# Query columns fetched from device memory in place of a TensorE transpose and a ScalarE copy, in a graph attention kernel

## The chip, the core and the metric

The kernel runs on one core of a Trainium2 chip. The core has five engines that run side by side, each in the order of its own program: TensorE (PE; its weight loads are listed as PEld), VectorE (DVE), ScalarE (ACT), GpSimd (POOL) and SyncE (SP), which here issues all but two of the transfers. They meet through semaphores. The metric is the device time of one execution in microseconds; before the change the median of three runs is 1442.3 us (1441.92 to 1442.65).

## The reference

Two layers over 128 graphs of 128 nodes with 256 features:

```python
h = relu(layernorm(x));  x = x + (adj @ (h @ W0) + b0)
h = relu(layernorm(x))
proj = (h @ fc_w + fc_b) split into 8 heads of 256
q = proj @ q_w + q_b;    k = proj @ k_w + k_b          # one number per node and head
masked = leaky_relu(q + k.T + (1 - adj) * -1e9, 0.01)
out = softmax(masked) @ proj                            # per head
x = x + sigmoid(concat(out) @ fp_w + fp_b + h)
```

All of it is in 32-bit floats. The attention logit of nodes n and m in a head is the sum of a query that depends on n and a key that depends on m.

## The kernel before

The 128 graphs are taken as 64 pairs (J = 2 graphs each). Weights are folded before the loop: `fc_w` and `fp_w` become one matrix `m` per head, so that a pair needs only projections into `gbank` (`project`) and an attention-weighted sum into `ybank` (`attend`). Most products are made of three matmuls on a high and a low part of each operand (helper `split`, L350). For each pair the engines do this:

- TensorE makes a block of 16 key and 16 query rows per pair, and the low part of each, in `kq` (`queries_keys`, L431). ScalarE copies the low part out (`kq_rows`, L1206), VectorE adds high, low and bias into `kq_sb` (`keys_queries`, L784). In `kq_sb` graph j has 8 key rows and 8 query rows from row 32 j on, 128 nodes wide.
- Keys are needed as rows on every partition: SP writes `kq_sb` to device memory (`keys_out`, L248) and reads the key rows back, repeated over all 128 partitions (`keys_in`, L260, 1 MB). GpSimd adds them to the mask (`mask_keys`, L1556).
- Queries are needed as columns, one number per partition and head: TensorE transposes `kq_sb` (`turn_queries`, L437), and ScalarE copies 16 of its columns into `qs` (`queries`, L1213). VectorE adds them to the masked keys and takes the minimum (`mask_min`, L810).
- Then come the slope and the negated exponent (`leaky` L817, `exp` L1226), the reciprocal of the sum (`inverse` L822), `normalise` on GpSimd (L1563), the transpose of the attention weights on TensorE (`transpose_p`, L454), their high and low parts (L1233, L800) and `attend`. `project` is followed by its own high and low parts (`g_high` L1219, `g_low` L793), which free its bank for a later `project`.

The work of neighbouring pairs is interleaved. Its order on every engine is written out by hand: a start (`begin`), a loop body with three pairs a turn (`step` for pair i), and an end (`finish`). In the loop body SP issues `load(i)`, `keys_in(i - 4)`, `store(i - 6)` and `keys_out(i - 3)`. `load` waits until GpSimd has used up the buffer (L1546, L1548). Pair i + 1 gets its key and query rows while pair i is projected, and uses them one body later. Buffers for rows, keys and queries exist three times (U = 3), and key rows go through the three tensors `key_rows0` to `key_rows2`.

Of the kernel before, what the change touches and what calls it, by code (L numbers as in the profile page):

```python
# [10 lines left out]
P = 128  # L11
D = 256
DT = D // P
H = 8
J = 2
# [12 lines left out]
U = 3  # L28
# [12 lines left out]
def gnn_pair(nc, graph, identity, head_mask, row_coef, w0, bias0, fc_wT, fc_b, qk_w, q_b, k_b, fp_w, fp_b, out):  # L41
# [9 lines left out]
    with ExitStack() as ctx:  # L51
# [87 lines left out]
        kq, kqT = bank1[0:2 * HALF, 0:J * P], bank1[:, J * P:J * P + P]  # L139
# [6 lines left out]
        s_loaded, s_stored, s_rows, s_keys = sem("s_loaded"), sem("s_stored"), sem("s_rows"), sem("s_keys")  # L146
        g_ones, g_none, g_qk = sem("g_ones"), sem("g_none"), sem("g_qk")
# [10 lines left out]
        pe_kq, a_kq, v_kq, pe_kqT, a_qs = [sem(n) for n in ("pe_kq", "a_kq", "v_kq", "pe_kqT", "a_qs")]  # L158
# [42 lines left out]
        def _(sp):  # L201
# [42 lines left out]
            def keys_out(p, q):  # L244
                sp.wait_ge(v_kq, p + 1)
                if has(p - 1):
                    sp.wait_ge(s_rows, 16 * p)
                sp.dma_start(key_rows[q][0:HALF + H], kq_sb[q][0:HALF + H]).then_inc(s_rows, 16)  # L248

            def keys_in(p, q):  # L250
# [4 lines left out]
                sp.wait_ge(a_qs, p + 1)  # L255
# [12 lines left out]
            def begin():  # L268

                load(0, 0)  # L270
                weights_out(0)
                weights_in(0)
                load_w0()
                weights_out(1)
                weights_in(1)
                weights_in(2)
                weights_out(2)
                weights_out(3)
                weights_in(3)
                load_bias0()  # L280
                load(1, 1)
                weights_out(4)
                weights_in(4)
                weights_out(5)
# [3 lines left out]
                load(2, 2)  # L288
                load_output_bias()
                load(3, 0)  # L290
                load(4, 1)
                load_identity()
                keys_out(0, 0)
                keys_in(0, 0)
                keys_out(1, 1)
                keys_in(1, 1)
                keys_out(2, 2)
                keys_in(2, 2)
                load(5, 2)
                load(6, 0)  # L300
                store(0)
                keys_out(3, 0)
                keys_in(3, 0)
                keys_out(4, 1)
                store(1)
                keys_in(4, 1)
                load(7, 1)
                load(8, 2)
                keys_out(5, 2)
                store(2)  # L310

            def step(i, q):
                load(i, q)
                keys_in(i - 4, (q + 2) % U)
                store(i - 6)
                keys_out(i - 3, q)

            def finish():

                keys_in(59, 2)  # L320
                store(57)
                keys_out(60, 0)
                load(63, 0)
                keys_in(60, 0)
                store(58)
                keys_out(61, 1)
                keys_in(61, 1)
                store(59)
                keys_out(62, 2)
                keys_in(62, 2)  # L330
                keys_out(63, 0)
                keys_in(63, 0)
                store(60)
# [6 lines left out]
            steady(sp, step, 9, 63)  # L340
# [4 lines left out]
        def _(pe):  # L345
# [127 lines left out]
            def begin():  # L473

                warm()
                fold(0)
                fold(1)
                key_query_bias()
# [4 lines left out]
                fold(5)  # L483
                fold(6)
                transform(0, 0)
# [3 lines left out]
                fold(10)  # L489
                aggregate(1, 1)  # L490
                fold(11)
# [9 lines left out]
                turn_queries(0, 0)  # L501
# [6 lines left out]
                aggregate(3, 0)  # L508
                h_ready(1)
                queries_keys(1, 1)  # L510
                project(0, 0, 4)
                output_bias()
                turn_queries(1, 1)
                project(0, 0, 6)
                project(0, 0, 5)
                project(0, 0, 7)
                transpose_h(2, 2)
# [636 lines left out]
        def _(act):  # L1154
# [53 lines left out]
            def queries(p, q):  # L1208
                act.wait_ge(pe_kqT, p + 1)
                if has(p - U):  # L1210
                    for n in range(J * NC):
                        act.wait_ge(v_mx[n], p - U + 1)
# [653 lines left out]
```

## Time and profile before

| What | Value |
|---|---|
| median of 3 runs | 1442.3 us |
| the profiled execution, its own time | 1442.27 us |
| its span in the trace | 1440.5 us |
| around the span | 1.8 us |
| granted TensorE clock, mean | 1.0 (of 2.4 GHz) |
| busy PE, DVE, ACT, POOL | 99%, 89%, 78%, 76% |
| DMA queue of SP, share of 16 engines | 23.9% |

The page gives for each engine its busy time and instructions; "idle before" is time in which the engine stood still ahead of an instruction, and the name behind the arrow is what ended it. In a timeline a row is an instruction with its start and its length; matmuls are pipelined, so a matmul's share of TensorE is the distance from its start to the next start and not its length. SPq is SP's queue of transfers: its length is that of the issue, not that of the transfer.

### The profile page before, as it was taken

How to read it: one execution, taken by the hardware profiler on the slowest of the kernel's cores; microseconds unless marked ns; L12 is line 12 of the kernel's file. 1: busy time of each engine (PE TensorE's matmuls, PEld its weight loads, DVE VectorE, ACT ScalarE, POOL GpSimd, SP SyncE). 2: the span in 40 equal slices, each digit the busy share in tenths (PEclk: the TensorE clock that was granted, in tenths of full speed). 3: DMA queues.
4: the chain of work that ended last, by engine and by line, in shares of the span. 5: the costliest groups of instructions: out<-in, count | busy, mean ns of one | idle time of the engine just before them, and what ended most of it. 6: DMA issues, size and time to landing. Idle time of an engine off the chain costs nothing.

```text
span 1440.5 us, 31578 instructions
## 1 busy us (share of the span) xinstructions
PE 1430.7 (99%) x9112; PEld 1279.6 (89%) x9112; DVE 1281.4 (89%) x4394; ACT 1130.3 (78%) x3479; POOL 1100.9 (76%) x1295
## 2 busy tenths in 40 slices
PE   8999999999999999999999999999999999999998
PEld 7888889889889888898898898888988988988887
DVE  7988998988988988989889889889898898898996
ACT  4877787787787787877877877878778778778776
POOL 4778877778778778777787787787777777877864
PEclk9999999999999999999999999999999999999999
DMA  6313212212222122122122221221221222212201
GB/s 221 112 43 115 104 52 103 97 58 102 73 81 103 55 100 103 52 102 97 58 102 73 82 103 55 100 103 52 102 97 59 102 74 81 103 54 86 89 32 59
DMA packets 43115, 123.88 MB, mean 86 GB/s; under 512 B 4304, under 2 KB 9552, under 8 KB 43088
## 3 DMA queue, kind: packets, MB, share of 16 engines
q1 hardware_dynamic: 42800, 123.55, 23.9%
q8 instruction: 12, 0.20, 0.1%
q14 instruction: 15, 0.12, 0.0%
q10 hardware_dynamic: 288, 0.01, 0.0%
HBM read 105.46 MB, written 18.09 MB: 86 GB/s over the span
## 4 chain that ended last, share of the span: by engine, by line
PE 97%; DMA 2%; DVE 0%; issue 0%; SPq 0%; POOL 0%; ACT 0%; POOLq 0%; DVEq 0%; ACTq 0%
PE gbank L350 49%; PE ybank L350 25%; PE tbank L454 8%; PE bank L350 6%; PE bank L395 4%; PE bank L431 2%; PE bank L418 2%; DMA g_in<-graph_dram 1%; PE bank L437 0%; DMA ident<-identity_dram 0%; DVE att L810 0%; DMA out_dram<-ends 0%; SPq L205 0%; SPq L210 0%; POOL ends L1579 0%
## 5 line engine op out<-in xcount | busy, mean ns | idle before, releaser
L1556 POOL TENSOR_TENSOR att<-late,t_pos 128x512 f32<-128x512 f32 x256 | 331.0, 1294 | 133.3 <-PE tbank L454 129.3
L350 PE MATMUL gbank<-m_hi,hT_lo 128*128 128x512 f32 x1024 | 428.7, 419 | 0.0
L1226 ACT ACTIVATE att<-att 128x128 f32<-128x128 f32 x1024 | 397.9, 392 | 37.0 <-DVE att L817 32.3
L350 PE MATMUL gbank<-m_lo,hT_hi 128*128 128x512 f32 x1024 | 405.7, 396 | 0.0
L350 PE MATMUL gbank<-m_hi,hT_hi 128*128 128x512 f32 x1024 | 404.4, 395 | 0.0
L793 DVE TENSOR_TENSOR g_lo<-gbank,g_hi 128x512 fp32r<-128x512 f32 x512 | 342.5, 680 | 47.5 <-ACT g_hi L1219 42.7
L1563 POOL TENSOR_TENSOR att<-att,rinv 128x512 f32<-128x512 f32 x256 | 290.4, 1134 | 114.7 <-DVE rinv L822 114.5
L1219 ACT ACTIVATE g_hi<-gbank 128x512 fp32r<-128x512 f32 x512 | 291.0, 595 | 54.4 <-PE gbank L350 54.1
L810 DVE TENSOR_SCALAR_CACHE_REDUCE att<-att,qs 128x128 f32<-128x128 f32 x1024 | 291.7, 342 | 31.7 <-POOL att L1556 31.6
L350 PE MATMUL ybank<-g_hi,pT_lo 128*128 128x256 f32 x1016 | 292.3, 288 | 0.0
L1233 ACT ACTIVATE pT_hi<-tbank 128x512 fp32r<-128x512 f32 x256 | 153.3, 599 | 170.8 <-PE tbank L454 165.2
L350 PE MATMUL ybank<-g_hi,pT_hi 128*128 128x256 f32 x1016 | 287.0, 283 | 0.0
L350 PE MATMUL ybank<-g_lo,pT_hi 128*128 128x256 f32 x1016 | 286.9, 282 | 0.0
L350 PEld LDWEIGHTS gbank<-m_hi,hT_hi 128*128 128x128 f32 x1024 | 193.9, 189 | 44.1
L350 PEld LDWEIGHTS gbank<-m_lo,hT_hi 128*128 128x128 f32 x1024 | 193.9, 189 | 26.6
L350 PEld LDWEIGHTS gbank<-m_hi,hT_lo 128*128 128x128 f32 x1024 | 193.5, 189 | 26.0
L350 PEld LDWEIGHTS ybank<-g_hi,pT_lo 128*128 128x128 f32 x1016 | 193.2, 190 | 14.4 <-DVE pT_lo L800 0.2
L350 PEld LDWEIGHTS ybank<-g_lo,pT_hi 128*128 128x128 f32 x1016 | 193.8, 191 | 8.5
L1226 ACT ACTIVATION_READ_ACCUMULATOR att<-att 128x1 f32 x1024 | 194.5, 190 | 0.0
L350 PEld LDWEIGHTS ybank<-g_hi,pT_hi 128*128 128x128 f32 x1016 | 194.1, 191 | 0.0
L817 DVE SCALAR_TENSOR_TENSOR att<-att 128x516 f32<-128x516 f32 x256 | 185.5, 743 | 0.1
L800 DVE TENSOR_TENSOR pT_lo<-tbank,pT_hi 128x512 fp32r<-128x512 f32 x256 | 173.7, 679 | 8.1 <-ACT pT_hi L1233 6.1
(100 smaller groups left out, 2360.5 us busy)
## 6 DMA issues: line engine op xcount, KB each, us to landing
late<-key_rows SPq DMA_DIRECT2D x64, 1024.0 KB, 5.9
g_in<-graph_dram SPq DMA_DIRECT2D x64, 512.0 KB, 3.3
out_dram<-ends SPq DMA_DIRECT2D x63, 256.0 KB, 3.5
key_rows<-kq_sb SPq DMA_DIRECT2D x64, 20.0 KB
late<-fp_w_dram SPq DMA_DIRECT2D x4, 256.0 KB, 5.5
att<-fc_wT_dram SPq DMA_DIRECT2D x4, 256.0 KB, 5.6
ends<-fp_w_dram SPq DMA_DIRECT2D x2, 512.0 KB, 8.8
late<-fc_wT_dram SPq DMA_DIRECT2D x2, 512.0 KB, 9.7
```

The lines of the kernel that those rows point to most:

```text
L350: mm = pe.matmul(out_ap, w, m, start=first and n == 0, stop=last and n == len(terms) - 1)
L395: mm = pe.matmul(sums[:, j, dt, :], h0_f[q][:, j, dt * P:(dt + 1) * P], adjT_of(q)[:, j, :], start=True, stop=True)
L454: mm = pe.transpose(tbank[:, h * P:(h + 1) * P], att[j][c][:, h * P:(h + 1) * P], ident[:])
L793: dve.tensor_tensor(g_lo[j][:, s], bank[:], g_hi[j][:, s].bitcast(F32), ALU.subtract)\
L800: dve.tensor_tensor(pT_lo[j][:, hs, :], rows, pT_hi[j][:, hs, :].bitcast(F32), ALU.subtract)\
L810: r = dve.tensor_scalar(a[:, s], a[:, s], qs[q][:, j, c * HC + h:c * HC + h + 1], None, ALU.add, ALU.min, accum_out=a[:, CH + h:CH + h + 1])
L817: dve.scalar_tensor_tensor(out=a, in0=a, scalar=SLOPE, in1=a, op0=ALU.mult, op1=ALU.min)\
L1219: act.activation(g_hi[j][:, s], gbank[tenant(RING, RSIZE, n, p)[0]][:], ACT.Copy).then_inc(a_g[n], 1)
L1226: e = act.activation(a[:, s], a[:, s], ACT.Exp, scale=-1.0, bias=a[:, CH + h:CH + h + 1], accum_out=esum[j][c][:, h:h + 1])
L1233: act.activation(pT_hi[j][:, c * HC:(c + 1) * HC, :], rows, ACT.Copy).then_inc(a_pT[NC * j + c], 1)
L1556: gp.tensor_tensor(a, keys[q][:, j, c * HC:(c + 1) * HC, :], t_pos[q][:, j, :].unsqueeze(1).broadcast_to([P, HC, P]), ALU.add)\
L1563: gp.tensor_tensor(a, a, rinv[j][c][:].unsqueeze(2).broadcast_to([P, HC, P]), ALU.mult)\
```

## The change

`turn_queries` and `queries` go away, with their bank and semaphores. `keys_out` now writes 48 rows in place of 40, so that the query rows of the second graph are in device memory too, and a new `queries_in` on SP reads the query rows back, one transfer for each graph, with node and head exchanged: partition n gets eight single numbers that lie 512 bytes apart in device memory. It waits until `keys_out` of its pair has landed and until the third pair back has used its queries. `mask_min` waits for the transfer of its graph, `keys_queries` for those of the pair that had its buffer, and `transpose_h` for `v_kq` in place of `a_qs`. `keys_in` no longer waits for `a_qs`. The start and the end are written in a new order on all engines; in the loop bodies of PE and ACT the one call is missing, those of DVE and POOL are as they were, and SP's has one call more.

```diff
@@ SP
-                sp.dma_start(key_rows[q][0:HALF + H], kq_sb[q][0:HALF + H]).then_inc(s_rows, 16)
+                sp.dma_start(key_rows[q][0:HALF + ROWS], kq_sb[q][0:HALF + ROWS]).then_inc(s_rows, 16)
+
+            def queries_in(p, q):
+
+                sp.wait_ge(s_rows, 16 * (p + 1))
+                if has(p - 1):
+                    sp.wait_ge(s_queries[0], 16 * p)
+                    sp.wait_ge(s_queries[1], 16 * p)
+                if has(p - U):
+                    for n in range(J * NC):
+                        sp.wait_ge(v_mx[n], p - U + 1)
+                for j in range(J):
+                    rows = key_rows[q][j * HALF + H:j * HALF + ROWS].rearrange("h n -> n h")
+                    sp.dma_start(qs[q][:, j, :], rows, allow_slow_non_contiguous=True).then_inc(s_queries[j], 16)
 
             def keys_in(p, q):
...
-                sp.wait_ge(a_qs, p + 1)
...
             def step(i, q):
-                load(i, q)
-                keys_in(i - 4, (q + 2) % U)
-                store(i - 6)
-                keys_out(i - 3, q)
+                load(i + 3, q)
+                keys_in(i - 1, (q + 2) % U)
+                store(i - 3)
+                keys_out(i, q)
+                queries_in(i, q)
...
-            steady(sp, step, 9, 63)
+            steady(sp, step, 6, 60)
@@ PE
-                    pe.wait_ge(a_qs, p)
+                    pe.wait_ge(v_kq, p)
...
-            def turn_queries(p, q):
-                pe.wait_ge(v_kq, p + 1)
-                pe.transpose(kqT, kq_sb[q][:], ident[:]).then_inc(pe_kqT, 1)
...
                 project(i, q, 0)
-                turn_queries(i + 1, (q + 1) % U)
                 attend(i - 1, 1, 1)
@@ DVE
-                    dve.wait_ge(pe_kqT, p - U + 1)
+                    for j in range(J):
+                        dve.wait_ge(s_queries[j], 16 * (p - U + 1))
...
-                dve.wait_ge(a_qs, p + 1)
+                dve.wait_ge(s_queries[j], 16 * (p + 1))
@@ ACT
-            def queries(p, q):
-                act.wait_ge(pe_kqT, p + 1)
...
-                queries(i + 1, (q + 1) % U)
```

TensorE in the loop body, end of `project(i, q, 0)` and start of `attend(i - 1, 1, 1)`, before:

```order
723 L350 MATMUL gbank<-m_hi,hT_lo 128x512
724 L350 MATMUL gbank<-m_lo,hT_hi 128x512
725 L350 MATMUL gbank<-m_hi,hT_hi 128x512
726 L437 MATMUL bank<-ident,kq_sb 128x128 [waits v_kq]
727 L350 MATMUL ybank<-g_hi,pT_lo 128x256 [waits v_g3,v_pT3]
728 L350 MATMUL ybank<-g_lo,pT_hi 128x256
```

The same place in the changed kernel, where `split` is L374:

```order
717 L374 MATMUL gbank<-m_hi,hT_lo 128x512
718 L374 MATMUL gbank<-m_lo,hT_hi 128x512
719 L374 MATMUL gbank<-m_hi,hT_hi 128x512
720 L374 MATMUL ybank<-g_hi,pT_lo 128x256 [waits v_g3,v_pT3]
721 L374 MATMUL ybank<-g_lo,pT_hi 128x256
722 L374 MATMUL ybank<-g_hi,pT_hi 128x256
```

One matmul and its wait are gone; all else stands as before.

SP in the loop body, one pair, before (ISA and REGISTER_ALU rows are waits and their arithmetic):

```order
61 L238 DMA g_in<-graph_dram 128x1024
62 L252 REGISTER_ALU
63 L260 DMA late<-key_rows 128x2x1024
64 L242 ISA
65 L242 DMA out_dram<-ends 128x512
66 L248 DMA key_rows<-kq_sb 40x128
```

The same of the changed kernel:

```order
74 L239 DMA g_in<-graph_dram 128x1024
75 L273 DMA late<-key_rows 128x2x1024
76 L243 ISA
77 L243 DMA out_dram<-ends 128x512
78 L249 DMA key_rows<-kq_sb 48x128
79 L253 REGISTER_ALU
80 L262 DMA qs<-key_rows 128x8x1 x2
```

The two query transfers stand behind the pair's `keys_out` and ahead of the next body's load and keys.

SP in the start, from the load of pair 1 on, before:

```order
10 L238 DMA g_in<-graph_dram 128x1024
11 L210 DMA ends<-fp_w_dram 128x4x256
12 L205 DMA late<-fc_wT_dram 128x1024
13 L210 DMA ends<-fp_w_dram 128x4x256
14 L205 DMA late<-fc_wT_dram 128x1024
15 L225 DMA kqb<-q_b_dram 8x1
16 L222 DMA kqb<-k_b_dram 8x1
17 L238 DMA g_in<-graph_dram 128x1024
18 L228 DMA c_row<-fp_b_dram 128x256
19 L238 DMA g_in<-graph_dram 128x1024 x2
20 L219 DMA ident<-identity_dram 128x128
```

In the changed kernel, from the load of pair 2 on:

```order
15 L239 DMA g_in<-graph_dram 128x1024
16 L211 DMA ends<-fp_w_dram 128x4x256
17 L206 DMA late<-fc_wT_dram 128x1024
18 L226 DMA kqb<-q_b_dram 8x1
19 L223 DMA kqb<-k_b_dram 8x1
20 L239 DMA g_in<-graph_dram 128x1024
21 L220 DMA ident<-identity_dram 128x128
22 L239 DMA g_in<-graph_dram 128x1024
23 L229 DMA c_row<-fp_b_dram 128x256
```

The loads of pairs 1 and 2 stand ahead of more of the weights than before, and the identity stands behind three later loads in place of four. For pairs 0 to 3 `queries_in` stands behind `keys_in`.

## Rows read from the trace of the kernel before

**Rows 1.** The page, part 1: busy time, share and instructions of each engine.

```profile
PE 1430.7 (99%) x9112; PEld 1279.6 (89%) x9112; DVE 1281.4 (89%) x4394; ACT 1130.3 (78%) x3479; POOL 1100.9 (76%) x1295
```

**Rows 2.** The page, part 4: the chain that ended last, by engine.

```profile
PE 97%; DMA 2%; DVE 0%; issue 0%; SPq 0%; POOL 0%; ACT 0%; POOLq 0%; DVEq 0%; ACTq 0%
```

**Rows 3.** Timeline of PE at the transpose: start, length, instruction.

```profile
698.74 0.40 PE L350 MATMUL gbank<-m_hi,hT_hi 128*128 128x512 f32 x1
698.97 0.27 PE L437 MATMUL bank<-ident,kq_sb 128*128 128x128 f32 x1
699.00 0.36 PE L350 MATMUL ybank<-g_hi,pT_lo 128*128 128x256 f32 x1
699.20 0.28 PE L350 MATMUL ybank<-g_lo,pT_hi 128*128 128x256 f32 x1
...
718.14 0.28 PE L350 MATMUL ybank<-g_hi,pT_lo 128*128 128x256 f32 x1
718.26 0.28 PE L350 MATMUL ybank<-g_lo,pT_hi 128*128 128x256 f32 x1
```

**Rows 4.** Groups of instructions, PE and ACT: count, busy, mean ns, idle.

```profile
L437 PE MATMUL bank<-ident,kq_sb 128*128 128x128 f32 x64 | 17.5, 274 | 0.2 <-DVE kq_sb L784 0.2
L1213 ACT ACTIVATE qs<-bank 128x16 f32<-128x16 f32 x64 | 11.3, 177 | 0.3 <-PE bank L437 0.3
```

**Rows 5.** Timeline of SP's transfers, one pair of the loop.

```profile
696.34 0.30 SPq L248 DMA_DIRECT2D key_rows<-kq_sb  x1
700.74 0.34 SPq L238 DMA_DIRECT2D g_in<-graph_dram  x1
701.26 0.37 SPq L260 DMA_DIRECT2D late<-key_rows  x1
```

**Rows 6.** Timeline of SP's transfers, the first pair.

```profile
31.93 0.31 SPq L248 DMA_DIRECT2D key_rows<-kq_sb  x1
33.26 0.37 SPq L260 DMA_DIRECT2D late<-key_rows  x1
```

**Rows 7.** DMA queues from 0 to 8 us: packets, MB, share of 16 engines.

```profile
q10 hardware_dynamic: 288, 0.01, 2.2%
```

**Rows 8.** DMA from 697.0 to 697.4 us, in 40 slices of 10 ns.

```profile
DMA  0000000000172553919535223030000000000000
...
DMA packets 50, 0.02 MB, mean 51 GB/s; under 512 B 10, under 2 KB 50, under 8 KB 50
...
q1 hardware_dynamic: 50, 0.02, 19.0%
```

**Rows 9.** Stretch of 1.3 us: last three numbers are clock, DMA share, GB/s.

```profile
700.70:702.00 1.30, 1.30 (x9) 1.13 (x8) 1.28 (x2) 0.84 (x2) 1.30 (x2) 1.00 0.31 60
```

**Rows 10.** DMA packets from 4 to 5 us.

```profile
DMA packets 359, 0.32 MB, mean 318 GB/s; under 512 B 143, under 2 KB 272, under 8 KB 359
```

**Rows 11.** The page, part 6: count, KB each, us to landing.

```profile
late<-key_rows SPq DMA_DIRECT2D x64, 1024.0 KB, 5.9
```

**Rows 12.** Timelines of POOL, DVE and PE in the loop, where keys are used.

```profile
708.49 1.28 POOL L1556 TENSOR_TENSOR att<-late,t_pos 128x512 f32<-128x512 f32 x1
...
715.22 1.30 POOL L1556 TENSOR_TENSOR att<-late,t_pos 128x512 f32<-128x512 f32 x1 [2.12 <-PE tbank L454]
...
711.22 0.34 DVE L810 TENSOR_SCALAR_CACHE_REDUCE att<-att,qs 128x128 f32<-128x128 f32 x1
...
712.28 1.46 DVE L793 TENSOR_TENSOR g_lo<-gbank,g_hi 128x512 fp32r<-128x512 f32 x2
...
714.81 0.47 PE L350 MATMUL gbank<-m_hi,hT_lo 128*128 128x512 f32 x1
```

**Rows 13.** Timeline of PE in the start; then the chain that ended last there.

```profile
20.57 1.16 PE L395 MATMUL bank<-g_in,h_f 128*128 128x128 f32 x8 [1.19 <-ACT h_f L1185]
...
27.75 0.63 PE L418 MATMUL bank<-ident,h 128*128 128x128 f32 x4 [1.66 <-DMA ident<-identity_dram]
...
24.35 3.26 DMA ident<-identity_dram
```

More of the change, by code:

```diff
@@ L287, in begin @@
                 load_key_bias()
-                load(2, 2)
+                load(3, 0)
+                load_identity()
+                load(4, 1)
                 load_output_bias()
-                load(3, 0)
-                load(4, 1)
-                load_identity()
                 keys_out(0, 0)
                 keys_in(0, 0)
+                queries_in(0, 0)
                 keys_out(1, 1)
+                load(5, 2)
                 keys_in(1, 1)
+                queries_in(1, 1)
                 keys_out(2, 2)
                 keys_in(2, 2)
-                load(5, 2)
+                queries_in(2, 2)
                 load(6, 0)
+                load(7, 1)
                 store(0)
@@ L332, in finish @@
                 keys_in(63, 0)
+                queries_in(63, 0)
                 store(60)
@@ L489, in begin @@
                 fold(10)
+                fold(11)
                 aggregate(1, 1)
-                fold(11)
                 fold(12)
@@ L511, in begin @@
                 project(0, 0, 4)
+                project(0, 0, 6)
+                aggregate(3, 0)
+                transpose_h(2, 2)
                 output_bias()
-                turn_queries(1, 1)
-                project(0, 0, 6)
                 project(0, 0, 5)
                 project(0, 0, 7)
-                transpose_h(2, 2)
                 transpose_p(0, 0, 0)
@@ L541, in begin @@
                 project(1, 1, 7)
-                aggregate(4, 1)
                 attend(1, 0, 1)
@@ L639, in finish @@
                 project(62, 2, 1)
+                attend(61, 1, 0)
                 transpose_p(61, 1, 1)
-                attend(61, 1, 0)
                 h_ready(63)
@@ L1077, in finish @@
-                mask_min(61, 1, 1, 1)
+                g_low(61, 3)
                 leaky(61, 1, 1)
-                g_low(61, 3)
                 inverse(61, 1, 0)
-                pT_low(61, 0, 0)
+                g_low(61, 0)
                 residual0(63, 0)
                 stats1(63, 0)
-                inverse(61, 1, 1)
                 mean1(63, 0)
-                g_low(61, 0)
+                pT_low(61, 0, 1)
                 mask_min(62, 2, 0, 0)
-                pT_low(61, 0, 1)
+                leaky(62, 0, 0)
@@ L1111, in finish @@
+                leaky(62, 1, 1)
+                inverse(62, 0, 1)
                 inverse(62, 1, 0)
                 pT_low(62, 0, 0)
-                g_low(62, 0)
+                inverse(62, 1, 1)
+                mask_min(63, 0, 0, 0)
+                pT_low(62, 0, 1)
+                leaky(63, 0, 0)
                 g_low(62, 5)
                 g_low(62, 4)
-                pT_low(62, 0, 1)
+                g_low(62, 7)
+                g_low(62, 6)
+                pT_low(62, 1, 0)
+                inverse(63, 0, 0)
@@ L1117, in finish @@
                 mask_min(63, 0, 0, 1)
-                mask_min(63, 0, 0, 0)
-                pT_low(62, 1, 0)
-                g_low(62, 7)
-                leaky(63, 0, 0)
-                g_low(62, 6)
+                g_low(63, 1)
+                g_low(63, 2)
+                pT_low(62, 1, 1)
                 leaky(63, 0, 1)
                 mask_min(63, 0, 1, 0)
-                pT_low(62, 1, 1)
-                inverse(63, 0, 0)
+                leaky(63, 1, 0)
+                inverse(63, 0, 1)
@@ L1206, in kq_rows @@
                 act.activation(kq_low[:], kq[HALF:HALF + ROWS], ACT.Copy).then_inc(a_kq, 1)
-            def queries(p, q):
-                act.wait_ge(pe_kqT, p + 1)
-                if has(p - U):
-                    for n in range(J * NC):
-                        act.wait_ge(v_mx[n], p - U + 1)
-                act.activation(qs[q][:], kqT[:, 0:J * HALF].rearrange("p (j r) -> p j r", j=J)[:, :, H:ROWS], ACT.Copy)\
-                   .then_inc(a_qs, 1)
             def g_high(p, n):
@@ L1271, in begin @@
                 fold_high(7)
-                u_none()
                 h0_relu(1, 1)
```

533 lines of the change are left out of this document (262 added, 271 removed).

## Prediction

> **What bounds the kernel now.** I read the page's part 1 first. TensorE is busy for 1430.7 of 1440.5 us, and the next engine, VectorE, for 89% [rows 1]. The chain of work that ended last says the same in another way: 97% of it is TensorE and 2% transfers, nothing else reaches 1% [rows 2]. So a change is worth what it takes off TensorE's stream of instructions, as long as no other engine or transfer comes late, and what it does to the start, where that 2% of transfers lies. Then I read the timelines of one pair in the loop, engine by engine; a pair takes 22 us. In the stretch I read, no matmul of the loop waits; the waits are on the other engines, GpSimd's 2.12 us for TensorE's transposes among them [rows 12].
>
> **Removed: the transpose on TensorE.** Its 274 ns [rows 4] are a length and not its price. In the timeline the last matmul of the projection starts at 698.74, the transpose at 698.97, the first matmul of `attend` at 699.00 and the second at 699.20. From the transpose's start to the second matmul of `attend` that is 0.23 us. At the other place of the pair where `attend` follows a projection directly, the first matmul starts at 718.14 and the second at 718.26, 0.12 us later [rows 3]. The transpose costs 0.23 - 0.12 = 0.11 us a pair, and 64 of them [rows 4] 7.0 us. All of it is on the path. For the gain to be kept no wait of TensorE may have been just met: the nearest that I found is the projection at 714.81, which needs its bank from the second `g_low` that ends at 712.28 + 1.46 = 713.74, 1.07 us earlier [rows 12]. That is ten times the 0.11 us that TensorE arrives earlier in each pair, and the other engines, fed by TensorE, move with it.
>
> **Removed: the copy on ScalarE.** 64 copies of 177 ns are 11.3 us [rows 4], on an engine busy for 78% [rows 1] and not in the chain [rows 2]. I cost it at nothing: TensorE's stream hides it. The semaphores that it set (`a_qs`) go with it; what waited for them (`transpose_h`, `keys_in`) was not in the chain either.
>
> **Added: the two query transfers.** This is the part that can lose. Per pair they move 2 x 128 x 8 = 2048 numbers in runs of one; over 16 DMA engines that is 128 packets for each engine, if each number is one packet.
>
> When do they start? `keys_out` is issued at 696.34 [rows 5]. In the start SP waits for it with nothing else in the way, and goes on 33.26 - 31.93 = 1.33 us after its issue [rows 6]. So `queries_in` is issued at about 697.67, twice 0.35 us by the issues around it [rows 5]. The first packets of `keys_out` show about 0.8 us behind its issue (from the tenth slice on, 697.1) [rows 8]; so the query packets run from about 698.4.
>
> What comes behind them? On SP's own program the load, at 700.74, and the keys, at 701.26 [rows 5]; SP stands free for them, since the query issues end at about 698.4. Their packets share SP's queue. DMA engines are busy for 0.31 of 1.3 us between 700.7 and 702.0 [rows 9], which is 0.4 us and puts the load's first packets at about 701.6. So there are 3.2 us in which the queues are empty today. Query packets fit into them if one takes up to 3.2 / 128 = 25 ns of its engine.
>
> What if they don't fit? Load and keys come later by the excess. The keys land 5.9 us after their issue [rows 11], at 707.2; GpSimd asks for them at 708.49, 1.3 us later. Its `mask_keys` ends at 709.77, and VectorE, which is busy until then, takes it up at 711.22, 1.45 us later. Behind that `mask_min` stand the two `g_low` with the 1.07 us of room worked out above [rows 12]. In all 1.3 + 1.45 + 1.07 = 3.8 us, so TensorE stands still only once query packets fill 3.2 + 3.8 = 7.0 us, that is 55 ns each. GpSimd's own order has room for it in its 2.12 us of waiting at 715.22 [rows 12]. The queries themselves are wanted at 711.22, far behind 698.4 + 7.0.
>
> What does a packet cost? The trace has no run of 4 bytes to columns. The nearest rows are the two small weight transfers on ScalarE's queue, 288 packets (16 or 64 bytes, and semaphores) that filled 2.2% of 8 us on 16 engines: 2.8 us, 9.8 ns each [rows 7]. `keys_out`, rows of 512 bytes, filled 19% of 0.4 us on 16 engines with 50 packets, 24 ns each; by its slices it took 0.26 us for 5 packets on each of 10 engines, 52 ns from one to the next, the slow end [rows 8]. Counted over all engines at once, 359 packets went through in one microsecond [rows 10]; at that rate 2048 take 5.7 us, which equals 45 ns an engine. The fast end is then 128 x 9.8 ns = 1.3 us, the slow end 128 x 52 ns = 6.7 us. I take the fast end, by the row nearest in size. Both are below 7.0 us, so both cost nothing at the end of the chain; the slow end is only 0.3 us away from costing something, and 55 ns is no bound of the hardware, so the far side stays in the range.
>
> The Trainium skill speaks against such a transfer: "DMA: Bandwidth & Descriptors", in the section Rules for kernel authors, says that a strided last dimension lowers to one descriptor for each element and should be rearranged, and its Specifications that below 512 bytes a transfer is a read, a modification and a write. The 9.8 ns of [rows 7] show no such doubling for loads of 16 and 64 bytes; if it came on top of the 512-byte row's time, that is the first rival below.
>
> `keys_out` carries 48 rows for 40, 4 KB more; at 24 ns a packet that is nothing that can be seen.
>
> **The start.** TensorE waits 1.19 us at 20.57 for the normalised input of pair 1 and 1.66 us at 27.75 for the identity, whose transfer runs from 24.35 to 27.6 behind the loads of pairs 1 to 4 [rows 13]. In the new order the load of pair 1 is issued three transfers earlier, one more fold stands before `aggregate(1)`, and the identity stands ahead of the load of pair 4. Both waits should shrink; at most 1.19 + 1.66 = 2.85 us. The last weights, though, now stand behind the load of pair 2, and the folds that need them come earlier, so a part can come back as a wait for weights. I take 2.0 us, ends 0 and 2.9. Against it: for pairs 0 to 3 the query transfers stand behind 1 MB of keys, so pair 0's queries land with or just behind its keys; at 22 us a pair and with projections to do meanwhile I give that 1 us at most, inside the same ends. The end of the kernel has a new order but no wait of TensorE that it could remove; I take 0, plus or minus 1 us.
>
> **The sum.** Against the profiled execution's 1442.27 us (span 1440.5 and 1.8 around it, 0.03 from the median): 1442.3 - 7.0 - 0 + 0 - 2.0 = 1433.3 us.
>
> **Rivals.**
> - The query packets become the bound. Place: SP's queue between `keys_out` and `keys_in`. It decides from 55 ns a packet. Each further 10 ns are 1.28 us a pair, in some 60 pairs of the loop 77 us, because a pair's keys are then late each time and VectorE, in its order, makes the next pair's rows later too. Against it: both rows of small packets. For it: the slow end is at 52 ns. A 512-byte packet alone is (1.22 us - 10 x 9.8 ns) / 40 = 28 ns [rows 7, 8]. If each number cost twice that and a little, 58 ns: 0.4 us a pair, +24 us, about 1458 us; more is possible. Chance 0.18.
> - The transpose's 0.11 us come back as waits: TensorE, 0.5% faster in each pair, meets a chain through ScalarE, VectorE and GpSimd that was in step with it by chance and not by its lead. Against it: the room of 1.07 us. Time: 1442.3 less the start's 0 to 2, say 1441.5 us. Chance 0.08.
> - Only the loop gains, the start does not: 1442.3 - 7.0 = 1435.3 us. For it: the weights. Chance 0.20.
> - That the change doesn't do what it says I can exclude: the transpose is gone from TensorE's order.
>
> **How the numbers follow.** The forecast has a chance of 0.54; its own range is 1431 to 1436.5 us (start and end together -2.9 to +1, a little for the 0.11). A measurement of this kernel can tell about 0.2%, 2.9 us, from no change. Faster: forecast and start-rival, less a little for a bad start or end, 0.73. Within 0.2%: the second rival and the edge of the first, 0.09. Slower: 0.18. The range runs from 1430.5 to 1445 us; above it lies most of the first rival, about 0.15, below it 0.03.
>
> **What would show it.** In the changed profile: no matmul on `kq_sb`; the distance from the projection's end to `attend`'s second matmul 0.35 us at both places; a pair in 21.9 us in place of 22.0; some 131,000 packets more under 512 bytes, and the DMA queue's share up by about 64 x 1.3 / 1440 = 6 points at the fast end, 30 at the slow end; `keys_in` still landing about 5.9 us after its issue. Waits of VectorE's `mask_min` for the query transfers, of GpSimd's `mask_keys` for the keys, and of projections for `g_low` would show the first rival; a period of 22.0 us without such waits the second.

## The result, and the profile after

The changed kernel takes 1435.33 us (median of 5 runs, 1434.24 to 1435.71) against 1442.3 us (1441.88 to 1442.65) before: ratio 0.995, 95% interval 0.9936 to 0.9964. It is faster, by 7.0 us. The forecast was 1433.3 us, 2.0 us too low; the measured time lies inside its range of 1430.5 to 1445 us, and it is the number of the third rival, 1435.3 us, "only the loop gains".

The profiled execution took 1434.97 us, of which 1432.8 are its span. Its page, part 1, 3 and 4 (engines; the queue of transfers of SP; the chain by engine), against [rows 1, 2]:

```profile
PE 1423.2 (99%) x9048; PEld 1274.6 (89%) x9048; DVE 1286.3 (90%) x4394; ACT 1124.7 (78%) x3415; POOL 1102.0 (77%) x1295
q1 hardware_dynamic: 176816, 124.35, 29.6%
PE 96%; POOL 1%; DMA 1%; DVE 1%; issue 1%; ACT 0%; SPq 0%; POOLq 0%; ACTq 0%
```

TensorE has 64 instructions fewer and stays the bound. Its timeline at the two places of [rows 3]:

```profile
694.04 0.39 PE L374 MATMUL gbank<-m_hi,hT_hi 128*128 128x512 f32 x1
694.27 0.28 PE L374 MATMUL ybank<-g_hi,pT_lo 128*128 128x256 f32 x1
694.39 0.28 PE L374 MATMUL ybank<-g_lo,pT_hi 128*128 128x256 f32 x1
...
713.10 0.39 PE L374 MATMUL gbank<-m_hi,hT_hi 128*128 128x512 f32 x1
...
713.45 0.28 PE L374 MATMUL ybank<-g_lo,pT_hi 128*128 128x256 f32 x1
```

From the projection's last matmul to the second of `attend` it is now 0.35 us at both; at the first of them it was 0.46 us. From one `queries_keys` to the next a loop pair takes 21.893 us in place of 22.006.

SP's timeline for one pair, against [rows 5], and what the transfers took to land (page, part 6: count, KB each, us), against [rows 11]:

```profile
691.64 0.32 SPq L249 DMA_DIRECT2D key_rows<-kq_sb  x1
693.08 0.99 SPq L262 DMA_DIRECT2D qs<-key_rows  x2
696.06 0.36 SPq L239 DMA_DIRECT2D g_in<-graph_dram  x1
696.51 0.38 SPq L273 DMA_DIRECT2D late<-key_rows  x1
...
late<-key_rows SPq DMA_DIRECT2D x64, 1024.0 KB, 6.0
...
qs<-key_rows SPq DMA_DIRECT2D x128, 4.0 KB, 2.5
```

A query transfer takes 0.5 us of SP to issue and lands after 2.5 us; the keys still go out 4.9 us behind `keys_out` and land after 6.0. In the stretches behind the query issues (the last three numbers are clock, DMA share, GB/s) the single numbers take up to 0.95 of the DMA engines and are gone before the load and the keys come:

```profile
694.00:694.50 0.50, 0.50 (x4) 0.42 (x4) 0.50 (x5) 0.13 (x3) 0.50 (x1) 1.00 0.30 2
694.50:695.00 0.50, 0.50 (x7) 0.50 (x6) 0.50 (x4) 0.50 (x1) 0.41 (x2) 1.00 0.95 7
...
695.50:696.00 0.50, 0.50 (x7) 0.50 (x6) 0.50 (x2) 0.00 (x0) 0.42 (x3) 1.00 0.41 3
696.00:697.00 1.00, 1.00 (x7) 0.86 (x6) 1.00 (x2) 0.66 (x2) 1.00 (x3) 1.00 0.00 0
```

GpSimd takes up the keys at the same points of the pair and waits the same 2.12 us as in [rows 12]:

```profile
703.68 1.28 POOL L1553 TENSOR_TENSOR att<-late,t_pos 128x512 f32<-128x512 f32 x1
...
710.41 1.30 POOL L1553 TENSOR_TENSOR att<-late,t_pos 128x512 f32<-128x512 f32 x1 [2.12 <-PE tbank L474]
```

VectorE never waits for a query transfer. The start is where the two traces differ most. These are all waits of TensorE behind the first 1.2 us and over 0.25 us, to be read against [rows 13]:

```profile
6.79 0.20 PE L400 MATMUL ybank<-ones,b_rows 128*16 128x2 f32 x2 [1.16 <-DVE b_rows L724]
10.68 1.16 PE L419 MATMUL bank<-g_in,h_f 128*128 128x128 f32 x8 [0.56 <-ACT h_f L1198]
46.25 0.66 PE L474 MATMUL tbank<-ident,att 128*128 128x128 f32 x4 [1.10 <-POOL att L1560]
116.66 0.63 PE L442 MATMUL bank<-ident,h 128*128 128x128 f32 x4 [0.51 <-ACT h L1208]
1317.99 0.66 PE L474 MATMUL tbank<-ident,att 128*128 128x128 f32 x4 [0.28 <-POOL att L1560]
```

Taken at the first matmul of `queries_keys` of pairs 0, 6 and 63, the two profiled executions divide so (us):

| stretch | before | changed | difference |
|---|---|---|---|
| to pair 0 | 29.80 | 27.54 | -2.26 |
| pair 0 to 6 (start) | 114.31 | 114.71 | +0.40 |
| pair 6 to 63 (loop) | 1253.55 | 1247.49 | -6.06 |
| pair 63 to the end of the span | 42.84 | 43.06 | +0.22 |
| around the span | 1.77 | 2.17 | +0.40 |
| all | 1442.27 | 1434.97 | -7.30 |

Up to pair 0 the order of the work is the same in every kernel below that has the new orders, and yet pair 0 starts anywhere from 26.8 to 28.0 us in their ten profiles. So the first difference, -2.26, is known to about half a microsecond only.

### The profile page after: what moved, and what is told of

Its sections match the earlier page's. It is cut to its first block, busy times and chain, and to the rows that moved or that the text cites. A ratio compares the mean times of both kernels' runs of the same rounds, so it can differ in the third digit from the quotient of the medians.

```text
span 1432.8 us, 31561 instructions
## 1 busy us (share of the span) xinstructions
PE 1423.2 (99%) x9048; PEld 1274.6 (89%) x9048; DVE 1286.3 (90%) x4394; ACT 1124.7 (78%) x3415; POOL 1102.0 (77%) x1295
## 3 DMA queue, kind: packets, MB, share of 16 engines
q1 hardware_dynamic: 176816, 124.35, 29.6%
## 4 chain that ended last, share of the span: by engine, by line
PE 96%; POOL 1%; DMA 1%; DVE 1%; issue 1%; ACT 0%; SPq 0%; POOLq 0%; ACTq 0%
PE gbank L374 49%; PE ybank L374 25%; PE tbank L474 8%; PE bank L374 6%; PE bank L419 4%; PE bank L455 2%; PE bank L442 2%; PE gbank L394 1%; DMA late<-key_rows 0%; POOL att L1560 0%; DMA qk<-qk_w_dram 0%; DVE att L823 0%; POOL att L1553 0%; DVE att L830 0%; DMA out_dram<-ends 0%
## 5 line engine op out<-in xcount | busy, mean ns | idle before, releaser
L374 PE MATMUL gbank<-m_hi,hT_lo 128*128 128x512 f32 x1024 | 428.7, 419 | 0.0
L374 PE MATMUL gbank<-m_lo,hT_hi 128*128 128x512 f32 x1024 | 405.0, 396 | 0.0
L374 PE MATMUL gbank<-m_hi,hT_hi 128*128 128x512 f32 x1024 | 404.7, 395 | 0.0
L374 PE MATMUL ybank<-g_hi,pT_lo 128*128 128x256 f32 x1016 | 287.3, 283 | 0.0
L374 PE MATMUL ybank<-g_hi,pT_hi 128*128 128x256 f32 x1016 | 287.0, 282 | 0.0
L374 PE MATMUL ybank<-g_lo,pT_hi 128*128 128x256 f32 x1016 | 286.9, 282 | 0.0
L374 PEld LDWEIGHTS gbank<-m_hi,hT_hi 128*128 128x128 f32 x1024 | 193.4, 189 | 44.6
L374 PEld LDWEIGHTS gbank<-m_lo,hT_hi 128*128 128x128 f32 x1024 | 193.8, 189 | 27.1
L374 PEld LDWEIGHTS gbank<-m_hi,hT_lo 128*128 128x128 f32 x1024 | 193.3, 189 | 25.6
L374 PEld LDWEIGHTS ybank<-g_hi,pT_lo 128*128 128x128 f32 x1016 | 193.3, 190 | 11.6 <-DVE pT_lo L813 0.2
L374 PEld LDWEIGHTS ybank<-g_lo,pT_hi 128*128 128x128 f32 x1016 | 193.6, 191 | 10.9
L374 PEld LDWEIGHTS ybank<-g_hi,pT_hi 128*128 128x128 f32 x1016 | 194.1, 191 | 0.0
L830 DVE SCALAR_TENSOR_TENSOR att<-att 128x516 f32<-128x516 f32 x256 | 192.5, 770 | 0.2
L813 DVE TENSOR_TENSOR pT_lo<-tbank,pT_hi 128x512 fp32r<-128x512 f32 x256 | 173.7, 678 | 6.8 <-ACT pT_hi L1238 4.8
```

The source lines that it names most:

```text
L374: mm = pe.matmul(out_ap, w, m, start=first and n == 0, stop=last and n == len(terms) - 1)
L813: dve.tensor_tensor(pT_lo[j][:, hs, :], rows, pT_hi[j][:, hs, :].bitcast(F32), ALU.subtract)\
L830: dve.scalar_tensor_tensor(out=a, in0=a, scalar=SLOPE, in1=a, op0=ALU.mult, op1=ALU.min)\
```

## The experiments

Each was measured beside the kernel before on its own chip, which took 1442.1 to 1442.2 us every time. "Changed" stands for the changed kernel, 1435.33 us.

### The transposes put back into the changed kernel, read by nobody (e2)

```diff
+            def turn_queries(p, q):
+                pe.wait_ge(v_kq, p + 1)
+                pe.transpose(kqT, kq_sb[q][:], ident[:]).then_inc(pe_kqT, 1)
```

It is called where it stood before in the loop, and at matching places of the new start and end; `keys_queries` waits for `pe_kqT` again.

> The changed kernel with the transpose of kq_sb put back on TensorE at its old places, with its wait for v_kq; nobody reads what it writes, ScalarE's copy stays away and the queries still come by the transfers. Theory (TensorE's stream is the bound and the transpose takes 0.11 us of it): 22.0 us a pair, 64 x 0.11 = 7.0 us more than the changed kernel, 1442.3 us. Rival (the gain came from ScalarE's 11.3 us of copies or from the waits that went): 21.9 us a pair and 1435.3 us.

Measured: 1443.42 us (1442.76 to 1444.46, 11 runs), ratio to before 1.0008 (0.9999 to 1.0017), 8.1 us above changed. The pair is back at 22.01 us: 0.11 us each is the price of the transpose on TensorE, 7.1 us for 64. ScalarE's copies stay away here, and the period is that of the kernel before all the same: the copies were worth nothing in the loop, and the rival fails. The last microsecond is a wait of the transpose itself in the start, where its rows are not ready yet; the expectation did not have it:

```profile
55.21 0.33 PE L462 MATMUL bank<-ident,kq_sb 128*128 128x128 f32 x1 [1.05 <-DVE kq_sb L811]
```

### The new way of the queries in the old orders (e1)

```diff
                 keys_out(0, 0)
+                queries_in(0, 0)
                 keys_in(0, 0)
```

and so for every pair; all other orders are those of before, without the two calls that are gone.

> The new mechanism in the old order: begin, step and finish of every engine as before the change, with turn_queries and queries taken out and queries_in put right behind every keys_out. Theory (the transpose's 0.11 us a pair is the whole effect, and the new order of the start and the end is worth about nothing): a pair takes 21.89 us as in the changed kernel, the start waits 1.2 and 1.7 us for pair 1 and for the identity as before, and the time is 1435 to 1436.5 us. Rival (the new order is what gained the 7 us, the mechanism is neutral): 22.0 us a pair and about 1442 us. Second rival (the mechanism gains more, and the new order gives part of it back): below 1434.5 us.

Measured: 1438.9 us (1437.11 to 1439.42, 10 runs), ratio 0.9975 (0.9965 to 0.9984). A miss. The loop pair is 21.89 us, as expected; the start loses. TensorE waits 2.07 us there, and then the granted clock (third number from the end) falls to 0.50, which is the level of 1.2 GHz. The timeline of GpSimd and TensorE, and the stretches:

```profile
41.31 1.30 POOL L1553 TENSOR_TENSOR att<-late,t_pos 128x512 f32<-128x512 f32 x1 [1.70 <-DMA late<-key_rows]
...
50.59 0.66 PE L474 MATMUL tbank<-ident,att 128*128 128x128 f32 x4 [2.07 <-POOL att L1560]
...
51.00:52.00 1.00, 1.00 (x10) 1.00 (x9) 1.00 (x3) 0.72 (x2) 0.00 (x0) 0.82 0.63 225
52.00:53.00 1.00, 1.00 (x7) 1.00 (x7) 1.00 (x4) 1.00 (x3) 0.23 (x1) 0.50 0.01 4
...
54.00:55.00 1.00, 1.00 (x7) 1.00 (x6) 1.00 (x2) 0.86 (x6) 1.00 (x1) 0.50 0.00 0
55.00:56.00 1.00, 1.00 (x11) 1.00 (x11) 0.06 (x1) 0.00 (x0) 1.00 (x2) 0.97 0.00 0
```

By these stretches the lower level lasts 3.4 us. GpSimd waits for the keys of pair 0, issued at 35.37 us behind 1.00 us of query issues. From pair 1 to pair 2 it is 14.46 us in place of 11.68. Two of the ten runs took 1437.1 to 1437.2 us, the others 1438.5 to 1439.4, as if the clock fell in most and not in all; only one of them has a trace, so that is not shown.

### The same with the keys ahead of the queries in SP's start (e5)

```diff
-                queries_in(0, 0)
                 keys_in(0, 0)
+                queries_in(0, 0)
```

and so for pairs 1 to 3.

> The new way of the queries in the old orders (as in e1), but in the start, for pairs 0 to 3, the transfer that reads the keys (late) is issued ahead of the two query transfers. In e1 the keys of pair 0 were issued at 35.37 us, behind 1.00 us of query issues, and GpSimd waited 1.70 us for them at 41.31; the TensorE wait of 2.07 us at 50.59 hangs on that chain. Theory (the start was slower in the old orders because the query issues stand ahead of the keys): the keys of pair 0 are issued 1.1 us earlier, the wait at 50.59 falls to 1.0 (0.9 to 1.2), pair 2 and 3 gain nothing, the time is 1437.8 us (1437.2 to 1438.2) against 1438.9. Rival (the place of the keys in SP's queue has nothing to do with it; what remains of the new start is the order on TensorE, ScalarE and VectorE): the wait stays at 2.0, 1438.9.

Measured: 1436.24 us (1435.61 to 1436.29, 5 runs), ratio 0.9958 (0.9944 to 0.9971): 2.7 us below e1, where 1.1 us was expected (a miss). The two ran on different chips, with the kernel before at the same time on both.

```profile
33.70 0.37 SPq L273 DMA_DIRECT2D late<-key_rows  x1
34.11 1.09 SPq L262 DMA_DIRECT2D qs<-key_rows  x2
...
39.42 3.77 POOL L1553 TENSOR_TENSOR att<-late,t_pos 128x512 f32<-128x512 f32 x3 [0.38 <-DMA late<-key_rows]
...
48.69 0.66 PE L474 MATMUL tbank<-ident,att 128*128 128x128 f32 x4 [0.75 <-POOL att L1560]
```

The wait falls from 2.07 to 0.75 us, which is the expected term (1.0 expected), and the clock stays at 1.00 behind it: pair 1 to pair 2 takes 11.89 us, 2.57 less. The wait gives 1.32 of that; the other 1.25 us fit what TensorE lost at the lower clock, at most half of 3.4 us. So some 1.1 us of query issues ahead of the keys cost 2.6 us of this stretch. What is left between this kernel and the changed one is 0.9 us (1436.24 against 1435.33); between it and the next kernel below, which has the new orders and the keys first everywhere, it is 2.6 us.

### The keys ahead of the queries everywhere, in the new orders (e3 and e11)

```diff
             def step(i, q):
                 load(i + 3, q)
                 keys_in(i - 1, (q + 2) % U)
+                queries_in(i - 1, (q + 2) % U)
                 store(i - 3)
                 keys_out(i, q)
-                queries_in(i, q)
```

The same is done for pairs 4, 5 and 59, and inside `queries_in` the waits for the pair that had the buffer are put first.

> The changed kernel with queries_in of a pair behind its keys_in, in the loop and for every pair, in place of ahead of load and keys. Theory (both places lie in spare time: keys then land without anything ahead of them, the queries 1 to 2 us behind them, before VectorE has done what stands ahead of mask_min): 21.89 us a pair, the half microsecond that pair 4's keys cost in the start is gone, 1434.8 to 1435.3 us. Rival (the queries have little room there: packets of single numbers behind 1 MB): mask_min waits for them, TensorE's matmuls start late, 22.2 us a pair or more, above 1450 us.

> The kernel of e3 (the query transfers behind the keys in SP's queue, everywhere), beside the changed kernel on one chip. Theory (query issues ahead of the keys cost the changed kernel 0.5 us of TensorE's time at 116.7 us with what follows it, and 0.3 to 0.5 us near 1318 us): 1433.55 us again, 1.3 to 2.0 us below the changed kernel. Rival (the first difference was one between chips): less than 0.5 us between the two.

> The changed kernel itself, on the chip of the two other kernels of this call, for a direct comparison. 1435.3 us (1434.6 to 1435.7), from its first measurement.

Measured: 1433.55 us (1432.87 to 1434.25, 5 runs), ratio 0.9941 (0.9927 to 0.9954), and again 1433.65 us (1433.26 to 1434.16) beside the changed kernel on one chip, there 1435.08 us (1434.25 to 1435.52): 1.4 us apart, by the first measurements 1.8. It beats both kernels, by more than was expected of it. The trace says why. Changed issues the queries of pair 4 at 104.49 and its keys at 105.97; here the keys go first, 1.45 us behind `keys_out` in place of 3.07:

```profile
102.68 0.32 SPq L249 DMA_DIRECT2D key_rows<-kq_sb  x1
104.13 0.36 SPq L273 DMA_DIRECT2D late<-key_rows  x1
105.12 0.99 SPq L262 DMA_DIRECT2D qs<-key_rows  x2
```

In changed GpSimd waits for those keys, and TensorE 4 us later for what hangs on them (116.66, shown above):

```profile
105.97 0.36 SPq L273 DMA_DIRECT2D late<-key_rows  x1
...
112.75 1.29 POOL L1553 TENSOR_TENSOR att<-late,t_pos 128x512 f32<-128x512 f32 x1 [1.79 <-DMA late<-key_rows]
```

Here this wait is gone, and so is the one at 1318 us; the step from pair 4 to 5 is 18.55 in place of 19.25 us, and the one at the end of the loop 21.89 in place of 22.39. By these two steps 1.2 us. Over the whole stretches from pair 0 to 63 it is 1.0 us between the first two traces (114.20 and 1247.00 us here) and 0.9 us between the two taken on one chip.

The rest of the 1.4 to 1.8 us is not the order on SP: it lies ahead of pair 0, where both kernels do the same. The profiled run of e10 reaches pair 0 0.96 us later than that of e11, before any query is sent. TensorE waits there while the weights are folded, and then its granted clock falls for 3.4 us (a stretch, with the same columns as above):

```profile
6.72 0.20 PE L400 MATMUL ybank<-ones,b_rows 128*16 128x2 f32 x2 [1.79 <-DVE b_rows L724]
...
8.00:9.00 1.00, 1.00 (x3) 0.78 (x3) 0.93 (x2) 0.00 (x0) 0.86 (x3) 0.50 1.12 415
```

Three of the five runs of e10 have a mean clock of 0.998 and take 1435.1 to 1435.5 us, the two at 1.000 take 1434.25 and 1434.55; in e11 the three at 1.000 take 1433.3 to 1433.7 us. Compared at the same clock the order on SP is worth 0.9 us. That the slower runs owe it to this fall is shown by the trace of one of them alone.

### Two places of the changed start mended (e4)

```diff
+                mask_min(0, 0, 0, 0)
                 keys_queries(1, 1)
-                mask_min(0, 0, 0, 0)
@@ SP
+                keys_in(4, 1)
                 queries_in(4, 1)
-                keys_in(4, 1)
```

> The changed kernel with two swaps in the start: on VectorE mask_min(0, 0, 0, 0) stands ahead of keys_queries(1, 1) as before the change, and on SP keys_in(4, 1) ahead of queries_in(4, 1). Theory (the new order of the start gains 2.2 us up to the first transpose_h and loses 0.8 us in TensorE's wait at 46.25 us for pair 0's normalise and 0.5 us at 116 us behind pair 4's keys): TensorE's waits between 40 and 120 us go from 1.6 to 0.3 us and the time falls by 1.3 us to 1434.0 us. Rival (what waits there is set by other work, so that one wait takes the place of the other): 1435.3 us, with the same idle time on TensorE between 40 and 120 us.

Measured: 1434.66 us (1433.92 to 1435.34, 5 runs), ratio 0.9947 (0.9934 to 0.9961). The 1434.0 expected was missed; the median is 0.7 us below changed, with overlapping ranges. SP's half did what it should: no wait at 116 us, step 18.55. VectorE's half did nothing, the wait at 46.69 is still 1.10 us: the swap moved one `mask_min`, while `leaky`, which releases ScalarE, stayed behind both of them and `keys_queries`.

### VectorE's start reordered twice more (e6, e9), on top of e3

```diff
-                keys_queries(1, 1)
                 mask_min(0, 0, 0, 0)
-                mask_min(0, 0, 0, 1)
                 leaky(0, 0, 0)
+                keys_queries(1, 1)
+                mask_min(0, 0, 0, 1)
+                inverse(0, 0, 0)
                 leaky(0, 0, 1)
```

with `exp(0, 0, 0)` ahead of `ah_high(3, 0)` on ScalarE. The second one also puts `inverse(0, 0, 1)` and `pT_low(0, 0, 0)` ahead of `leaky(0, 1, 1)`.

> e3 (the query transfers behind the keys everywhere, 1433.55 us) with VectorE and ScalarE reordered at one place of the start: mask_min and leaky of the first quarter of pair 0 ahead of keys_queries(1, 1), its inverse ahead of leaky(0, 0, 1), and exp(0, 0, 0) ahead of ah_high(3, 0). In e4 only one mask_min was moved, and leaky, on which ScalarE's exp waits, stayed where it was (41.87 us), so the wait at 46.69 stayed 1.10. Theory (VectorE's order from 38 to 43 us sets the time of the first normalise): exp starts at 40.1 instead of 42.5, the normalise at 42.1 to 43 instead of 45.0, TensorE's wait at 46.04 (1.08 us) falls below 0.1, and all of it is kept: 1432.5 us (1432.2 to 1432.9). Rival (the 1.08 us comes back further on in the start, where VectorE is full): 1433.5, with a new wait of TensorE of about 1 us before 100 us.

> The kernel of the second start order, with three steps of VectorE moved once more for pair 0: inverse(0, 0, 1) and pT_low(0, 0, 0) ahead of leaky(0, 1, 1). There the wait of 1.08 us of TensorE at 46 us had gone and one of 1.03 us for pT_lo came up at 49.02 us, 1434.72 us. Theory (one VectorE order stands behind both waits): pT_lo is made at 47.2 in place of 48.28, the wait at 49.02 falls below 0.2 and the time goes 0.8 to 1.1 us below that kernel, 1433.8 us (1433.4 to 1434.1), level with the kernel that has only the queries behind the keys. Rival (VectorE has no room at all between 34 and 50 us, so that each wait taken out comes back at the next result that TensorE wants): another wait of about 1 us before 70 us, 1434.7.

Measured: 1434.72 us (1434.55 to 1435.8) and 1434.46 us (1434.14 to 1434.58), 5 runs each: both misses (1432.5 and 1433.8 expected), and both slower than the kernel they start from (e9 by 0.8 us on one chip). The wait at 46 us, 1.08 us in e3, is gone in e6, and two have taken its place:

```profile
42.27 0.63 PE L442 MATMUL bank<-ident,h 128*128 128x128 f32 x4 [0.57 <-issue]
...
49.02 0.39 PE L374 MATMUL ybank<-g_hi,pT_lo 128*128 128x256 f32 x1 [1.03 <-DVE pT_lo L813]
```

The first is the price of the edit itself: `transpose_h` at 42.27 waits by the program for `keys_queries(1, 1)`, which now stands behind `leaky` and ends at 42.17 us, in place of 39.06 in e3. In e9 it is still there, the one at 49.02 is gone, and the step from pair 2 to 3 grows from 31.31 to 31.78 us, with a wait of 0.31 at its begin. So each wait that was taken out came back elsewhere, as the rivals say, though not as one wait of 1 us. That VectorE has no room in this stretch is likely from this and not shown: an order that moves `leaky` up and leaves `keys_queries(1, 1)` where it was has not been tried.

### Four and twelve more query transfers a pair (e7, e8)

```diff
+                for r in range(4):
+                    rows = key_rows[q][r % J * HALF + H:r % J * HALF + ROWS].rearrange("h n -> n h")
+                    sp.dma_start(qx[:, r, :], rows, allow_slow_non_contiguous=True).then_inc(s_extra[r], 16)
```

ahead of the two real ones, in the changed kernel; `range(12)` in e8.

> The changed kernel with four more element-wise query transfers per pair (six in place of two), into a tile that nothing reads, issued ahead of the two real ones. Theory (a transfer of 1024 single numbers costs 0.5 us of issue and 9.5 ns a packet over 16 engines, 0.6 us): six take 3.0 us of issue and 3.7 us of packets, which fit before the keys are sent at 696.5 (the queries began at 693.1): the keys still land in time, 1435.3 us (1434.8 to 1436.5), the pair stays 21.9 us, packets 0.69 million, the queue's share up by another 17 to 18 points. Rival 1 of the prediction (single-number packets crowd the queue, 55 ns and more each when more of them stand in line): late lands 7 us or more after its issue and VectorE or GpSimd waits for it every pair, 1450 us or more.

> As the kernel with four more, but with twelve more (fourteen element-wise transfers a pair). Theory (0.5 us of issue, 0.6 us of packets each): 7.0 us of issue and 8.5 us of packets from 693.1 on, so the keys are issued near 700.3 in place of 696.5 and the packets ahead of them end near 701.8; the keys land at 706 to 708 in place of 702.5, GpSimd wanted them at 703.7: a wait of 2 to 4.5 us in each pair, of which TensorE feels between 0 and all: pair 22 to 26 us, 1440 to 1690 us, with GpSimd's mask_keys waiting for late in nearly every pair. Rival (the transfers are issued out of the way and packets of different transfers share the engines, so that even fourteen are hidden): 1435.3 us, pair 21.9 us.

Measured: 1451.9 us (1451.15 to 1454.07, 4 runs), ratio 1.0073 (1.0058 to 1.0089), and 1815.83 us (1807.67 to 1819.57, 4 runs), ratio 1.2582 (1.2551 to 1.2613). Both are misses in time: 16.6 us above the theory's 1435.3 and 126 us above its 1690. The 0.69 million packets expected of e7 were miscounted: they are 443,373, and the queue's share rises by 10.8 points. For e7 the theory holds in the loop and fails outside it. The loop pair is 21.88 us, although GpSimd waits for the keys in nearly every pair (first row: us in all, times, longest); TensorE pays in the start and at the end, where the pairs stand closer:

```profile
POOL att L1560 <- DMA late<-key_rows: 61.5, 57, 5.1
...
697.38 0.32 SPq L251 DMA_DIRECT2D key_rows<-kq_sb  x1
698.82 2.24 SPq L266 DMA_DIRECT2D qx<-key_rows  x4
701.10 1.54 SPq L269 DMA_DIRECT2D qs<-key_rows  x2
703.13 0.36 SPq L241 DMA_DIRECT2D g_in<-graph_dram  x1
703.58 0.38 SPq L280 DMA_DIRECT2D late<-key_rows  x1
...
120.63 1.02 PE L449 MATMUL bank<-ident,h 128*128 128x128 f32 x4 [3.86 <-ACT h L1215]
1326.34 1.12 PE L481 MATMUL tbank<-ident,att 128*128 128x128 f32 x4 [3.27 <-POOL att L1567]
1400.97 0.66 PE L449 MATMUL bank<-ident,h 128*128 128x128 f32 x4 [2.00 <-ACT h L1215]
```

Against the changed kernel the profiled run is 5.4 us longer between pairs 0 and 6 and 9.5 us from pair 6 to 63. The keys go out 703.58 - 697.38 = 6.2 us behind `keys_out`, 1.3 later than in changed (6.4 us at the median of the loop, 1.5 later). Six issues took 3.8 us where 3.0 were expected: with more of them in line an issue grows from 0.5 to 0.6 or 0.8 us. With fourteen, GpSimd's waits reach TensorE (waits of e8, same columns):

```profile
POOL att L1560 <- DMA late<-key_rows: 389.3, 58, 10.4
PE tbank L481 <- POOL att L1567: 173.7, 58, 8.9
```

A pair takes about 27.6 us, 5.7 more. TensorE stands still for 3.7 us of it (these 173.7 and another 40.4 us for `g_lo`, by 58). The mean clock of the whole run is 0.925, which is the lower level for about 270 us, and fits the other 2 us a pair. The keys went out 11.7 to 13.1 us behind `keys_out`, 12.2 at the median of the loop, 7.3 later than in changed: some 7.3 - 3.7 = 3.6 us of lateness stay hidden. It is a rough figure, since the clock stretches the pair as well.

## Why the prediction came out as it did

- **The transpose, -7.0 us: right.** 0.113 us a pair by the period, 0.46 to 0.35 us in the timeline, and 0.11 us again when it is put back.
- **The copy, 0: right.** ScalarE has 64 instructions and 5.6 us of busy time fewer, and e2, without the copies and with the transposes, has the period of the kernel before, 22.01 us.
- **The query packets, 0: right in the loop, at the fast end.** The queue's time rose from 23.9% of 1440.5 to 29.6% of 1432.8 us, times 16 engines by the 134,016 packets added: 9.5 ns each, against 9.8 taken from [rows 7] and 55 needed for the first rival. With four more transfers a pair it is 9.7 ns, with twelve 9.1. The rule that the prediction quotes from the Trainium skill ("DMA: Bandwidth & Descriptors", Rules for kernel authors), one descriptor for each element, is what the trace shows (133,504 packets more under 512 bytes); of an extra cost for the read and write back that the prediction quotes beside it, 9.5 ns a packet show nothing. The slow end of the prediction, 52 ns, was misread: in [rows 8] the first slice that is not 0 is the eleventh and the last the twenty-seventh, 0.17 us and not 0.26, so 34 ns. What the sum left out is the issue: 0.5 us each and not 0.35, and more in line. In the loop it is hidden, since SP waits for the load's buffer until 696.06 anyway.
- **The room, 3.8 us: about right, as a whole.** e7's 1.5 us are hidden in the loop, of e8's 7.3 about 3.6. How it divides is less sure: GpSimd was to have 1.3 us of it, and in e7 it waits 0.8 us at the median for keys that are 1.5 us later.
- **The start, -2.0 us: this step failed.** TensorE did reach pair 0 earlier by 2.26 us, and both waits named in the prediction are gone. But by pair 6 only 1.86 us were left, of which 0.7 are the transposes of six pairs: the start is worth 1.2 us. It gave 0.8 us back at 46.25 us, behind GpSimd's and VectorE's work on pair 0 (1.10 us of wait, 0.31 before; in the orders tried here it went only for others to come), and 0.5 at 116.66, where the query issues hold up the keys. The prediction looked for late query data ("at most 1 us") and not for what stands behind the query issues on SP: the keys. The loop has the load's wait as cover for them; start and end have none. One wait of that kind came at the end of the loop as well, 0.5 us. It takes the new orders too: before the change the keys of pair 4 also went out 2.88 us behind `keys_out` (106.56 - 103.68), in e1 3.17, and TensorE waited at neither place in either.
- **Around the span and behind the last pair, 0: off by +0.4 and +0.2 us.** The first is in all kernels without transposes (2.2 us against 1.8; 1.9 with the transposes back). What lies outside the span has no record, so its cause stays open.
- **The third rival, 1435.3 us,** has the right number for another reason: it held the weights to cost the start its gain. In the profiled run no matmul waits for them. In the ten profiles with the new orders, weights late or not, pair 0 starts at 26.8 to 28.0 us; in the three with the old ones at 29.8 to 30.7.
- **The first rival** needed slow packets. e7 and e8 show that its mechanism is there, late keys that GpSimd waits for, but it takes many more transfers, and comes through the issues on SP.

With the keys ahead of the queries the kernel takes 1433.6 us, what was predicted for the changed one. The order on SP was the missing term for about 1 of the 2 us, by the traces and by runs at the same clock. That the number agrees to 0.3 us is in part luck: this kernel still has the wait at 46 us and the 0.4 us around the span, and makes up for them with a larger gain up to pair 0 (2.67 and 2.96 us in its two traces).

## What to carry to other kernels

Here a transfer that replaced work of the bounding engine was free only where everything behind it on its queue could also be late. So, of such a transfer, ask whether everything behind it on its queue can also be late, and look first at what stands behind its issue, in the start and the end as well as in the loop. Where two transfers wait for the same data, issue first the one whose reader comes first in the chain that the bounding engine waits for (0.9 us here). The price of an instruction on a full TensorE is the distance from start to start with and without it (0.11 us here), not its length (0.27 us), and a wait of 2 us in its stream can cost more than its own length. Before a difference of 1 us between two kernels is explained, compare the stretch that both have in common: here 0.96 of 1.8 us between two profiles lay there.

## What the runs showed of the hardware

- Single 4-byte numbers to 128 partitions cost 9.1 to 9.7 ns of a DMA engine each (changed, e7, e8). A transfer of 1024 of them takes 0.5 us to issue, 0.6 to 0.8 with six in line and up to 1.2 at the end of fourteen, and lands after 2.5 to 2.8 us.
- After TensorE's wait of 2.07 us in e1 its clock was granted at 0.50 for 3.4 us, with a loss of another 1.25 us. It fell as long behind waits of 1.73 us (e4) and 1.79 us (e10), both in the start near 7 us, and of 3.86 us (e7), and for 6.8 us around one of 3.27 us (e7). After 1.10 us in the changed kernel, 1.59 in e3, 1.78 in e5 and 2.00 in e7 it stayed at 1.00. The length of the wait alone does not tell.
- VectorE's `leaky` and GpSimd's `mask_keys` or `normalise` hold each other up, and in these rows (e6) it is the one that starts later that pays. `leaky` begins at 39.97 while three `mask_keys` run; it takes 1.60 us, and they 3.78, no more than three of the 1.29 us that one takes elsewhere. The next `leaky` begins first and takes 0.69 us, which is also its time with nothing beside it, and `normalise` beside it takes 1.45 in place of 1.04 us. In the changed kernel 117 of the 256 `normalise` lie beside a `leaky`, with a median of 1.40 us:

```profile
37.23 3.78 POOL L1553 TENSOR_TENSOR att<-late,t_pos 128x512 f32<-128x512 f32 x3
...
39.97 1.60 DVE L830 SCALAR_TENSOR_TENSOR att<-att 128x516 f32<-128x516 f32 x1
43.40 0.69 DVE L830 SCALAR_TENSOR_TENSOR att<-att 128x516 f32<-128x516 f32 x1
...
43.54 1.45 POOL L1560 TENSOR_TENSOR att<-att,rinv 128x512 f32<-128x512 f32 x1 [0.70 <-DVE rinv L835]
```
